# First scores and maxima of three attention layers moved into the MLP ahead of each

## The reference

```python
x = _L0_xattn_ref(...)            # ends with MLP 0: gelu(h @ w_fc1 + b) @ w_fc2 + b + x
x = _L1_xattn_ref(x, ctx, ...)    # layer 1: 16 heads of 16, 256 queries x 256 keys; then MLP 1
x = _L2_xattn_ref(ctx, x, ...)    # layer 2: 16 heads, keys = 256 of ctx + 256 of x; then MLP 2
x = _L3_xattn_ref(x, ctx, ...)    # layer 3: 32 query heads of 8, 8 key heads, then a layer norm

# inside each layer
scores = q @ k.T * scale          # masked
attn = softmax(scores, axis=-1)
out = (attn @ v) @ w_o + b_o + residual
# each MLP (batch 4 x 256 rows, 256 wide, 1024 inside)
x + gelu(norm(x) @ W1 + b1) @ W2 + b2
```

## Time and profile before

| | us |
|---|---|
| median of 3 runs | 1248.57 |
| lowest, highest run | 1248.19, 1248.85 |
| the profiled execution's own time | 1249.79 |
| its span in the trace | 1248.4 |
| PE busy | 1203.5 |
| DVE busy | 888.7 |
| ACT busy | 779.8 |
| POOL busy | 598.9 |

### The profile page before, as it was taken

One profiled execution on the slowest core, in us unless ns is written; L12 is line 12 of the kernel. 1 busy time (PEld: TensorE's weight loads), 2 busy tenths in 40 slices (PEclk: granted clock), 3 DMA queues, 4 the chain that ended last, 5 costly groups with the idle time before them and its releaser, 6 DMA issues.

```text
span 1248.4 us, 27144 instructions
## 1 busy us (share of the span) xinstructions
PE 1203.5 (96%) x9940; PEld 1029.8 (82%) x9940; DVE 888.7 (71%) x2304; ACT 779.8 (62%) x1889; POOL 598.9 (48%) x966
## 2 busy tenths in 40 slices
PE   8999999999999999999989899999999899999997
PEld 7999999999999999999978665786675577666664
DVE  5887877779887777778865787537788464666764
ACT  4876666668876566666874566645676654555553
POOL 3784555548875555454862443504444131324333
PEclk9999999999999999999999999999999999999999
DMA  5540100013431001001420220122222012121100
GB/s 170 153 141 31 35 26 27 27 39 107 142 100 35 27 26 35 27 27 28 126 74 27 81 81 28 51 69 74 84 68 70 10 60 64 54 70 42 40 12 18
DMA packets 56820, 75.03 MB, mean 60 GB/s; under 512 B 11312, under 2 KB 30576, under 8 KB 56688
## 3 DMA queue, kind: packets, MB, share of 16 engines
q1 hardware_dynamic: 51568, 72.75, 19.1%
q0 software_dynamic: 5120, 0.56, 0.3%
HBM read 49.46 MB, written 1.05 MB: 40 GB/s over the span
## 4 chain that ended last, share of the span: by engine, by line
PE 80%; DVE 7%; issue 5%; ACT 4%; POOL 2%; DMA 1%; ACTq 0%; DVEq 0%; POOLq 0%
PE bank L125 19%; PE bank L127 18%; PE bank L126 18%; PE bank L2052 5%; PE bank L771 4%; PE bank L1999 3%; PE bank L2009 3%; PE bank L1985 2%; PE bank L2010 2%; PE bank L1981 1%; ACT PT L2126 1%; DMA Q<-rows 1%; PE bank L178 1%; PE bank L713 1%; PE bank L1736 1%
## 5 line engine op out<-in xcount | busy, mean ns | idle before, releaser
L1095 POOL TENSOR_SCALAR E<-E,rl 128x256 f32<-128x256 f32 x256 | 243.6, 962 | 210.2 <-DVE rl L980 210.2
L2126 ACT ACTIVATE PT<-bank 128x512 f32<-128x512 f32 x320 | 173.5, 594 | 92.6 <-PE bank L2010 56.0
L846 ACT ACTIVATE QTh<-bank,bqs 128x256 fp32r<-128x256 f32 x128 | 60.8, 475 | 156.3 <-PE bank L127 156.2
L2207 DVE CUSTOM_DVE_ANT_0 Em<-bank,M 128x256 bf16<-128x256 f32 x256 | 95.1, 420 | 53.8 <-PE bank L1985 22.3
L856 ACT ACTIVATE E<-bank,nm 128x257 f32<-128x257 f32 x256 | 119.5, 481 | 1.2 <-DVE nm L950 1.0
L984 DVE TENSOR_TENSOR PTl<-bank,PTh 128x512 fp32r<-128x512 f32 x128 | 88.0, 688 | 27.3 <-ACT PTh L868 26.8
L957 DVE SCALAR_TENSOR_TENSOR QTl<-bank,bqs,QTh 128x256 fp32r<-128x256 f32 x128 | 61.6, 481 | 64.0 <-ACT KT L847 63.2
L868 ACT CAST PTh<-bank 128x512 fp32r<-128x512 f32 x128 | 75.2, 588 | 43.2 <-PE bank L771 43.2
L2201 DVE TENSOR_REDUCE nm<-bank 128x1 f32<-128x512 f32 x128 | 83.3, 685 | 23.5 <-PE bank L1981 22.3
L950 DVE TENSOR_REDUCE nm<-bank 128x1 f32<-128x257 f32 x256 | 95.5, 414 | 3.6 <-PE bank L127 3.6
L1999 PE MATMUL bank<-Q,K 51*128 51x256 f32 (+1 forms) x640 | 85.2, 315 | 4.9 <-DMA Q<-rows 2.4
(11 more groups left out here) (438 smaller groups left out, 4382.2 us busy)
## 6 DMA issues: line engine op xcount, KB each, us to landing
stage<-in_wts SPq DMA_DIRECT2D x99, 256.0 KB, 3.3
U<-in_vrows SPq DMA_DIRECT2D x64, 256.0 KB, 2.7
K<-stage SPq DMA_DIRECT2D x48, 128.0 KB
Q<-stage SPq DMA_DIRECT2D x48, 128.0 KB
K<-stage SPq DMA_DIRECT2D x48, 64.0 KB
Q<-stage SPq DMA_DIRECT2D x48, 64.0 KB
K<-xh SPq DMA_DIRECT2D x16, 128.0 KB, 3.0
Q<-rows POOLq DMA_DIRECT2D x96, 4.0 KB, 1.7
```

The lines of the kernel that those rows point to most:

```text
L1095: m = pool.tensor_scalar(s.E[:, i % 3, t, 0:256], s.E[:, i % 3, t, 0:256], s.rl[:, r, t:t + 1], None, ALU.mult)
L2126: act.activation(s.PT[i % s.NPT][:, 2 * u:2 * u + 2, :].rearrange("p a b -> p (a b)"), s.STB[y][:], ACT.Exp).then_inc(S["t_ex"])
L2207: dve.tensor_tensor_reduce(out=s.Em[:, (2 * i + e) % 4], in0=bank[:, e * 256:e * 256 + 256], in1=s.M3[:, j, e, :], scale=-1.0, scalar=3.4e ...
```

## The change

1. The scores by query of the first two steps of layer 1, and of the first three of layers 2 and 3, are issued inside the MLP ahead, by the table `EARLY`: behind PE's work of MLP steps 14 and 15 (layer 1) or 13, 14 and 15 (layers 2 and 3). DVE takes their maxima behind its work of the same steps. They use three banks of their own (`EB`). The matmuls of ones of those layer steps are gone, 8 groups in all; those of steps 2 to 4 (layer 1) or 3 and 4 stay.
2. The first group's maxima are turned in MLP step 16, copied by ACT at the MLP's end, and sent by POOL there, too.
3. The first batch's queries (and all that leads to them) come one MLP step earlier. In layer 1 norm, turn and scale now share a step. In layer 2 the tokens' turn and keys use another bank.
4. ACT's table load moves from step 3 to step 0. ACT's copies of ones in the layers (`ONES_AT`) move to later steps, and POOL's `ones_keys` for the second batch moves to step 3.

```diff
@@ mlp_pe
         for b, x in nxt.during(i):
             heads_prep_pe(c, nxt, b, x)
+        for n in nxt.early(i):
+            heads_early_pe(c, nxt, n)
+        if i == 16:
+            heads_turn_maxima(c, nxt, 0, 0)
@@ mlp_act, at the end
+    heads_rows_act(c, nxt, 0)
@@ mlp_dve, in step i
+        for n in nxt.early(i):
+            for k in nxt.in_step(n):
+                heads_maxima(c, nxt, k)
@@ mlp_pool, at the end
+    heads_parts_pool(c, nxt, 0)
+    heads_rows_pool(c, nxt, 0)
@@
 IN_MLP = {1: {...
-              8: ["stats"], 9: ["norm"], 10: ["turn", "scale"], 11: ["th", "tl", "res"], 12: ["q0", "q1", "qh", "ql"],
-              13: ["q_out", "stats+"], 14: ["norm+"], 16: ["turn+", "scale+"]},
+              8: ["stats"], 9: ["norm", "turn", "scale"], 10: ["th", "tl", "res"], 11: ["q0", "q1", "qh", "ql"],
+              12: ["q_out", "stats+"], 13: ["norm+"], 16: ["turn+", "scale+"]},
...
+EARLY = {1: {14: 0, 15: 1}, 2: {13: 0, 14: 1, 15: 2}, 3: {13: 0, 14: 1, 15: 2}}
@@ class Heads
+    def query_bank(self, n):
+        return self.EB[n % 3] if n < self.WD * self.E else self.SB[n % 3]
+    def asked(self, n):
+        return self.in_step(n) if n >= self.E else ()
@@
-ONES_AT = {1: {0: ("q", 1, 0), 1: ("q", 1, 1), 2: ("v", 1, 0), 4: ("q", 2, 0), 5: ("q", 2, 1), 6: ("v", 2, 0)},
-           2: {1: ("q", 1, 0), 2: ("q", 1, 1), 3: ("v", 1, 0), 4: ("v", 1, 1)}, 3: {1: ("v", 1, 0)}}
+ONES_AT = {1: {3: ("v", 1, 0), 4: ("q", 1, 0), 5: ("q", 1, 1), 6: ("q", 2, 0), 7: ("q", 2, 1), 8: ("v", 2, 0)},
+           2: {5: ("q", 1, 0), 6: ("q", 1, 1), 7: ("v", 1, 0), 8: ("v", 1, 1)}, 3: {5: ("v", 1, 0)}}
+def heads_by_query(c, s, n, e):
...
+    if n < 3:
+        w.wait_ge(S["m_hf"], 4 * (l - 1) + 3)
+        w.wait_ge(S["m_x"], 4 * (l - 1) + 2)
+    elif first <= n < first + 3:
+        w.wait_ge(S["m_gelu"], 16 * l)
+        w.wait_ge(S["t_rows"], s.o["g"] + 1)
+        w.wait_ge(S["t_mx"], s.o["mx"] + first * k)
+    else:
+        w.wait_ge(S["t_mx"], s.o["mx"] + (n - 2) * k)
...
+def heads_early_pe(c, s, n):
+    if n == 0:
+        heads_ready(c, s, 0)
+    for e in (range(1) if s.l == 2 else range(2)):
+        for k in s.in_step(n):
+            heads_by_query(c, s, k, e)
@@ keep_busy
-        if n < s.L:
-            w.wait_ge(S["m_x"], 4 * (l - 1) + 2)
+        if s.E <= n < s.L:
+            w.wait_ge(S["t_mx"], s.o["mx"] + s.WD * s.E * (2 if l == 3 else 1))
             ones(s.STB[1], {1: 4, 2: 4, 3: 6}[l])
@@ heads_act
-        if n == s.L - 2:
+        if n == 0:
             w.wait_ge(S["neghalf"], 1)
             act.activation(c.tiny[:], c.neghalf, ACT.Exp)
@@ heads_pool
-    ones_keys(c, s, 1)
...
+        if n == 3:
+            ones_keys(c, s, 1)
```

More of the change, by code:

```diff
@@ L1257, in take_first @@
         self.qbs = sb("qbs", [128, 2], F32, self.above)
+        self.nm = self.main("nm", [128, 4, self.G, 2])
+        self.np = self.main("np", [128, 2, 2, 2, self.G // 2, 2], F32R)
+        self.rows = self.main("rows", [128, 2, 128], F32R)
+        if self.l == 3:
+            self.Em = self.main("Em", [128, 4, 256], BF16)
     def take_rest(self, c):
@@ L1356, in turned_by @@
     def turned_by(self, n):
-        return sum(len(self.turns_at(k)) for k in range(n + 1))
+        return 1 + sum(len(self.turns_at(k)) for k in range(n + 1))
     def attended_by(self, n):
@@ L1955, in heads_sp, with heads_ready, heads_turn_maxima @@
         w.wait_ge(S["st_out1"], 48)
+def heads_ready(c, s, b):
+    S, w, l = c.S, c.pe_w, s.l
+    for x in "qk":
+        w.wait_ge(S["dma_h" + x], 64 * s.spreads(b + 1))
+        w.wait_ge(S["dma_l" + x], 32 * s.spreads(b + 1))
+    if l == 2:
+        w.wait_ge(S["dma_hx"], 64 * (b + 1))
+        w.wait_ge(S["dma_lx"], 32 * (b + 1))
+    if l != 3:
+        w.wait_ge(S[f"dma_mask{b % 2}"], 32 * (2 * (l - 1) + b // 2 + 1))
+def heads_by_query(c, s, n, e):
+    S, pe, w, l = c.S, c.pe, c.pe_w, s.l
+    p, u, y = s.unit(n)
+    q, r = p % s.P, p // s.P % s.NR
+    at = s.at(q, y, s.R)
+    bank, first, k = s.query_bank(n), s.WD * s.E, 2 if l == 3 else 1
+    if n < 3:
+        w.wait_ge(S["m_hf"], 4 * (l - 1) + 3)
+        w.wait_ge(S["m_x"], 4 * (l - 1) + 2)
[5 more added lines that the diff above has]
+        w.wait_ge(S["t_mx"], s.o["mx"] + (n - 2) * k)
+    if l == 2:
+        pe.matmul(bank[:], s.Q[r][at, q, u * 128:u * 128 + 128], s.K[r][at, q, :], start=True, stop=True
+                  ).then_inc(S["t_s"])
+        return
+    z = pe.matmul(bank[:, 256 * e:256 * e + 256], s.Q[r][at, q // s.blocks, 128 * e:128 * e + 128],
+                  s.K[r][at, q // s.rp, :], start=True, stop=True)
+    if e == 1:
+        z.then_inc(S["t_s"])
+def heads_turn_maxima(c, s, g, attended):
+    S, pe, w = c.S, c.pe, c.pe_w
+    w.wait_ge(S["t_np"], s.o["g"] + g + 1)
+    w.wait_ge(S["t_rows"], s.o["g"] + g)
+    w.wait_ge(S["t_os"], s.o["os"] + attended)
+    pe.transpose(s.turned(g), f32(s.np[:, g % 2]).rearrange("p y a q t -> p (y a q t)"), c.ident[:]
+                 ).then_inc(S["t_rT"])
+def heads_early_pe(c, s, n):
[4 more added lines that the diff above has]
+            heads_by_query(c, s, k, e)
 def heads_pe(c, s, nxt):
@@ L2013, in fours @@
     def fours(n):
-        if n < s.T and n % s.TB == 0:
-            ready(n // s.TB)
-        if n < 2:
-            w.wait_ge(S["m_gelu"], 16 * l)
+        if 0 < n < s.T and n % s.TB == 0:
+            heads_ready(c, s, n // s.TB)
         for e in (range(1) if l == 2 else range(2)):
-            for k in s.in_step(n):
-                by_query(k, (e,))
+            for k in s.asked(n):
+                heads_by_query(c, s, k, e)
         for e in range(2):
@@ L2112, in heads_pe, with heads_rows_act @@
         for g in s.turns_at(n):
-            turn_maxima(g, n)
+            heads_turn_maxima(c, s, g, s.attended_by(n - 1))
     if l == 3:
         close_pe(c, s)
+def heads_rows_act(c, s, g):
+    S, w = c.S, c.act_w
+    w.wait_ge(S["t_rT"], s.o["g"] + g + 1)
+    if g >= 2:
+        w.wait_ge(S[f"dma_rows{g % 2}"], 32 * ((s.o["g"] + g) // 2))
+    c.act.copy(s.rows[0:4 * s.G, g % 2, :], s.turned(g)).then_inc(S["t_rows"])
 def heads_act(c, s, nxt):
@@ L2211, in heads_dve @@
+def heads_dve(c, s, nxt):
+    w, l = c.dve_w, s.l
     mlp_end(c, w, l - 1)
     for n in range(s.steps()):
-        for k in s.in_step(n)[:s.WD - 1]:
-            maxima(k)
+        for k in s.asked(n)[:s.WD - 1]:
+            heads_maxima(c, s, k)
         for b, x in s.preps(n - 1):
@@ new lines, in heads_parts_pool, with heads_rows_pool @@
+def heads_parts_pool(c, s, g):
+    S, pool, w = c.S, c.pool, c.pool_w
+    n, nm, np = s.o["g"] + g + 1, s.nm[:, g % 4].rearrange("p (q y) t -> p y q t", y=2), s.np[:, g % 2]
+    high, low = (np[:, 0], np[:, 1]) if s.l == 3 else (np[:, :, 0], np[:, :, 1])
+    w.wait_ge(S["t_mx"], s.mx((g + 1) * s.G))
+    w.wait_ge(S["t_rT"], n - 2)
+    pool.tensor_copy(high, nm).then_inc(S["t_nh"])
+    w.wait_ge(S["t_nh"], n)
+    pool.tensor_tensor(low, nm, f32(high), ALU.subtract).then_inc(S["t_np"])
+def heads_rows_pool(c, s, g):
+    S, pool, w = c.S, c.pool, c.pool_w
+    b, pair, n = g * s.G // s.nh, g * s.G % s.nh // 2, s.G // 2
+    w.wait_ge(S["t_rows"], s.o["g"] + g + 1)
+    if s.l == 3:
+        for a in range(2):
+            pool.dma_start(f32(s.Q[b % s.NR][s.R + a:s.R + a + 97:32, pair // 2, :]),
+                           f32(s.rows[8 * a:8 * a + 8, g % 2, :])).then_inc(S[f"dma_rows{g % 2}"], 16)
+        return
+    for y in range(2):
+        at = 64 * y + s.R
+        pool.dma_start(f32(s.Q[b % s.NR][at:at + 2, pair:pair + n, :]),
+                       f32(s.rows[4 * n * y:4 * n * y + 4 * n, g % 2, :])).then_inc(S[f"dma_rows{g % 2}"], 16)
```

139 lines of the change are left out of this document (41 added, 98 removed).

## The result

| | before | after |
|---|---|---|
| median, us | 1249.84 | 1252.31 |
| lowest to highest | 1247.76 to 1251.78 (20 runs) | 1247.77 to 1255.27 (20 runs) |
| ratio of the two | | 1.0020, 95% interval 1.0013 to 1.0027 |
| own time of the profiled execution | 1249.79 | 1250.95 |
| its span | 1248.4 | 1249.4 |

The change makes the kernel 2.5 us slower (1.6 to 3.4 by the interval). The forecast was 0.6 us slower, 1249.2 (on the 1249.84 of these runs 1250.4), and its own range went up to 1251: the sign held, the size did not, and the time lies outside the forecast's own range. The wide range of 1244.7 to 1252.8, which was drawn to take in slower rivals too, holds it near its upper end. After's runs spread over 7.5 us, before's over 4.0, and the profiled execution of after is 1.4 us quicker than its median. So the two traces show 1.0 to 1.2 us of the 2.5.

A forecast was written before the change was run, and what follows sets the result against it. PE was taken to bound the kernel, busy 1203.5 of 1248.4 us. Layers 1, 2 and 3 summed as -1.8 + 0.5 + 1.9 = +0.6 us, to 1249.2 us; own range 1247 to 1251, wide range 1244.7 to 1252.8.

The forecast's parts named there:

- The waits and their places: Layer starts and MLPs: layer 3's queries at 4.75 us, layer 1's at 5.9, layer 2's values at 16.8, MLP 1's gelu 0.95 later.
- 3.4 us of full list at half speed cost 1.7: Layer 3's start: PE's 4 us idle brings a clock fall, 3.4 us at half speed, costing 1.7 us.
- rival A: All three layers: waits shorter than thought, layer 3 keeps its clock, layer 2's copies fit in; 1244.7 us, chance 0.22.
- Layer 1: MLP 0 about 0.8 us later, step 5 at 11.95 instead of 14.55 behind time 0; net 1.8 us gained.
- Layers 1 and 2 together: Layer 1 gains 1.8 us and layer 2 loses 0.5, with the MLPs ahead of them counted in.
- Rival C: Layers 1 and 2: the clock falls there too, each costing 1.6 us, from a wait of some 1.7; 1252.4 us, chance 0.20.
- B: Removed groups of ones were pure cost and nothing waits behind them: -9.0 us, 1239.6 us, chance 0.04.
- Rival D: MLP step 13 or 14: first scores wait for their copies, 2 us in one layer; 1251.2 us, chance 0.04.
- Rival E: Table load's drain counts: 1.4 us more ahead of hTh in layer 3, 0.5 in layer 1; 1251.1 us, chance 0.04.

The follow-up runs named there:

- fill3: Changed kernel with 15 matmuls of ones put into PE's 4.0 us wait at layer 3's start: 1248.11 us, ratio 0.9985 to the kernel before.
- undo3: Changed kernel with layer 3's early scores, maxima's turn, ones and table load put back in the layer: 1248.41 us, ratio 0.9983 to the kernel before.
- table3: Changed kernel with layer 3's ACT table load at step 2 instead of step 0: 1247.44 us, ratio 0.9978 to the kernel before.
- noones: Changed kernel without the seven groups of ones it kept in steps 0 to 4: 1246.80 us, ratio 0.9986 to the kernel before.
- all_noones: Changed kernel with layer 3's load later, nine ones in its wait, layer 2's copies of ones earlier, without the seven kept groups: 1242.61 us, ratio 0.9932.

## Why the prediction was nearly right, and where it was not

**The waits and their places: right.** The queries of layer 3 at 4.73 (4.75), PE idle there for 4.02 us, the load ahead of hTh, a fall of the clock behind it, the keys and queries of layer 1 at 2.44 and 5.98, layer 2's step 5 at 7.36 and values at 16.70, the gelu delayed by 1.07 in MLP 1: each within 0.1 or 0.2 us of the working.

**The term that was mis-sized** is "3.4 us of full list at half speed cost 1.7" in layer 3. I took the length of the fall from the window behind the 1.77 us wait and gave it to a wait more than twice as long. The earlier trace rows had a longer one too, the 6.7 us in layer 1, and I used it for rival A only. Measured: some 10 us at half speed and 4.0 us lost (4.2 beside fill3). Put in place of 1.7, the sum is +0.6 + 2.3 = +2.9 us, against 2.5 in the medians. undo3, fill3 and table3 each take the loss away again (4.4 to 5.2 us; table3 by a wait that is 1.5 us shorter and a fall of 3.4 us). That the fall comes in after's other executions too is seen in their mean granted clock: 0.989 over its 20, against 0.992 in fill3 and undo3 and 0.991 in table3. 0.003 of 1250 us is 7.5 us at half speed, which costs up to 3.8 us.

**Layer 1** was taken 0.9 us too well: step 5 at 12.81, not 11.95. The working summed the list from the queries on to 6.05 us and left out two waits that the kernel before has as well; its 6.93 us stood in the earlier trace rows.

**Layers 1 and 2 together** gave 2.1 us by the ratios (undo3, 1.0 to 3.1) where the working had 1.3. The traces show less: about 1.0 for layer 1, and for layer 2 a loss of some 0.5 when the falls that only before's execution had are left out. The rest of the 2.1 has no place in a trace. So that the corrected sum comes within 0.4 us of the measurement is partly luck.

**Rival C** put a longer clock loss in layers 1 and 2 and named 1252.4. The time agrees by chance, the place does not: layer 1's window at 708 to 720 is 0.72 before and after, and layer 2's start is at full clock. Nor does the clock decide at a wait of some 1.7 us: 1.77 us brought a fall in some traces and none in others, as the last section shows. The Trainium skill's warning (TensorE: Matmul & The Clock Gate, HAM oscillation), that waits between bursts make the next burst run cold, came true for layer 3 (a wait of 4.02 us, then a clock of 0.64) and not where I had placed it. fill3 bears it out from the other side: with the wait filled the burst kept its clock.

**Rival A** (waits shorter) and **B** (ones pure cost) fail as wholes. noones and all_noones show a part of B: the seven groups that the change kept stood ahead of ready work, and without them the layers' starts gave 3.9 and 3.6 us in all, with what was lost behind them taken off, about half of the groups' own 7.6 us. The kernel without them was 4.2 us faster in one case and no faster in the other.

**Rival D**, first scores that wait for their copies, did not happen: none of the scores inside the three MLPs waits in after's trace.

**Rival E**, the drain at a table load: hTh follows the load's first exponential at 1053.93, 0.11 us after that began at 1053.82. The 1.38 us which the Trainium skill adds (ScalarE: Activation LUTs, What ACT_TABLE_LOAD costs) do not show on this path; its 1.28 for the load does.
